# Selective scan: a fourth state of sixteen weighted on GpSimd, and C's rows split as 128x64 tiles

## The reference, cut to what matters

```python
xdbl = jnp.einsum('bld,de->ble', xc, W_xproj)
dt_r, Bm, Cm = xdbl[..., :8], xdbl[..., 8:24], xdbl[..., 24:]
dt = softplus(einsum(dt_r, W_dt) + b_dt)          # 512 steps x 256 channels
def step(h, inp):
    h = h * exp(dt_t[:, :, None] * A) + dt_t[:, :, None] * B_t[:, None, :] * u_t[:, :, None]
    y = jnp.einsum('bdn,bn->bd', h, C_t)          # sum over the 16 states n
    return (h, y)
y = (ys + xc * D_param) * silu(z)
out = x + einsum(y, W_out)
```

## Time and profile before

| | us |
|---|---|
| median of 3 runs (lowest, highest) | 2778.79 (2772.78, 2779.42) |
| the profiled execution's own time | 2771.78 |
| its span | 2770.0 |
| the scan, first recurrence to last weighting (900.4 to about 1330) | some 430 |

### The profile page before, as it was taken

How to read it: one execution, slowest core, us unless ns; L and a number is a source line. 1 busy time by engine, 2 the same in 40 slices (tenths; PEclk the granted TensorE clock), 3 DMA queues, 4 the chain that set the end, 5 groups by cost and what they waited for, 6 DMA issues and landing times. The chain is left out here.

```text
span 2770.0 us, 42642 instructions
## 1 busy us (share of the span) xinstructions
PE 2480.3 (90%) x13253; PEld 1589.3 (57%) x13280; DVE 1740.7 (63%) x4100; ACT 1433.8 (52%) x2908; POOL 1615.9 (58%) x1421
## 2 busy tenths in 40 slices
PE   7977787799578899997579899999999999999999
PEld 4756777687565344433379734444444445777776
DVE  4436444575424999999756599999999992211112
ACT  3431333334246877775334377777777774333333
POOL 4742555442364999999145376777767771997000
PEclk9988999899788999999889999999999999999999
DMA  9011333500012232322520068888888884000001
GB/s 295 25 35 49 109 107 108 165 1 24 26 40 73 93 98 91 96 97 88 175 80 25 14 142 196 192 191 191 191 195 187 194 193 100 9 16 9 8 8 31
DMA packets 148262, 274.82 MB, mean 99 GB/s; under 512 B 29003, under 2 KB 68694, under 8 KB 148038
## 3 DMA queue, kind: packets, MB, share of 16 engines
q1 hardware_dynamic: 135798, 251.75, 35.2%
q0 software_dynamic: 9088, 18.63, 2.4%
q10 hardware_dynamic: 3152, 1.71, 0.3%
HBM read 102.97 MB, written 24.58 MB: 46 GB/s over the span
## 5 line engine op out<-in xcount | busy, mean ns | idle before, releaser
L1784 POOL TENSOR_TENSOR l3a_p_all<-l3a_p_all,l3a_rden 128x1024 f32<-128x1024 f32 x256 | 483.7, 1893 | 202.2 <-DVE l3a_rden L1859 202.1
L1917 ACT ACTIVATE l3a_p_all<-l3a_p_all,l3a_low 128x512 f32<-128x512 f32 x512 | 364.3, 713 | 129.8 <-DVE l3a_low L1854 128.5
L1854 DVE CUSTOM_DVE_ANT_0 l3a_p_all<-bank,relative_bias 128x512 f32<-128x512 f32 x512 | 331.9, 686 | 53.9 <-PE bank L1983 30.5
L1867 DVE STREAM_TRANSPOSE l3a_blocks<-l3a_p_all 128x1024 f32<-128x1024 f32 x256 | 313.9, 1235 | 1.8 <-issue 1.8
L2784 POOL TENSOR_TENSOR l2a_dBu<-l2a_du,l2a_bs 128x1024 f32<-128x1024 f32 x128 | 298.5, 2352 | 17.4 <-DVE l2a_h L3020 16.2
L3020 DVE TENSOR_TENSOR_SCAN l2a_h<-bank,l2a_dBu 128x1024 f32<-128x1024 f32 x128 | 290.9, 2281 | 11.9 <-POOL l2a_dBu L2784 6.5
L1841 DVE SCALAR_TENSOR_TENSOR x<-bank,l3a_blocks,x 128x128 f32<-128x128 f32 x256 | 71.9, 344 | 336.5 <-PE bank L2058 336.3
L1932 ACT ACTIVATE relative_bias<-bank,l3a_b 128x512 f32<-128x512 f32 x224 | 153.3, 687 | 214.1 <-PE bank L2048 210.8
L1983 PE MATMUL bank<-l3a_kT,l3a_qT 64*128 64x512 f32 x1024 | 245.3, 607 | 3.1 <-DVE l3a_low L1854 2.6
L2009 PE MATMUL bank<-l3a_pT,l3a_v 128*64 128x512 f32 x1024 | 233.8, 598 | 0.1
L2048 PE MATMUL bank<-relative_xnT_all,relative_w_qk 128*128 128x512 f32 x512 | 231.0, 595 | 0.0
(11 more groups left out here) (532 smaller groups left out, 4964.3 us busy)
## 6 DMA issues: line engine op xcount, KB each, us to landing
l3a_pT<-l3a_blocks SPq DMA_DIRECT2D x1024, 128.0 KB
l2a_bs<-l2a_b_rows SPq DMA_DIRECT2D x128, 256.0 KB, 3.1
l0fe_wv<-expert_weights SPq DMA_DIRECT2D x71, 256.0 KB
by_place<-by_distance SPq DMA_DIRECT2D x16, 512.0 KB, 12.6
relative_bias<-by_place SPq DMA_DIRECT2D x16, 448.0 KB, 11.3
l2a_c_rows<-l2a_b_rows SPq DMA_DIRECT2D x24, 256.0 KB
expert_weights<-in_L_ffn_in_dram SPq DMA_DIRECT2D x1, 4096.0 KB, 29.1
l0f_answers<-l0f_y_rows SPq DMA_DIRECT2D x16, 256.0 KB, 5.2
```

Source lines behind the costliest of these rows:

```text
L1784: p_ready.by(pool.tensor_tensor(a, a, bcast(rden[g % 2][:, t, :], n_after=S), ALU.mult))
L1854: bk.drain(dve.tensor_tensor_reduce(p_of(g, t)[:, h, :], ps(job)[:], bias[:, u * 2 + h, b0:b0 + S], 1.0, 3.0e38, ALU.add, ALU.min, low[:, ...
L1867: ins = dve.transpose(out, p_of(g, t).rearrange("p h (k b j) -> p (h k) b j", b=Q, j=32))
L1917: ins = act.activation(a, a, ACT.Exp, bias=low[:, t, h:h + 1], scale=-1.0, accum_out=den[:, t, h:h + 1])
```

## The change

- Loads: C's 16 rows are read back from DRAM as one flat 128x64 tile (`c_flat`); SP issues this load for the first block before all, for block q + 1 ahead of the `bs` load of n = 5, and waits there for the store of `b_rows[q + 1]`.
- Splits: the rounding and subtracting run on 128x64, on C alone; three DMAs that ACT issues at n = 12 put the parts into `bc`. Their places in the orders move: ACT n = 1, 6, 11 to 6, 9, 12; POOL n = 5, 10 to 9, 12 (first block 7, 10 to 10, 13). PE's spread waits for these DMAs.
- SHARED becomes (0, 3, 6, 9), added at PE's steps 6, 9, 12, 15.
- POOL's step sizes are done at n = 11 and 12 in place of 12 and 13.

```diff
-        raw, dtr, left, mid = sb("raw", [2 * N, S]), sb("dtr", [R, S]), sb("left", [2 * N, S]), sb("mid", [2 * N, S], BF16)
+        raw, dtr = sb("raw", [2 * N, S]), sb("dtr", [R, S])
+        CUT = N * S // P
+        c_flat, c_left, c_parts = sb("c_flat", [P, CUT]), sb("c_left", [P, CUT]), sb("c_parts", [P, 3, CUT], BF16)
...
-        SHARED, LATER, ADDED_AT = (0, 3, 6), 4, {0: 6, 3: 12, 6: 13}
+        SHARED, LATER, ADDED_AT = (0, 3, 6, 9), 4, {0: 6, 3: 9, 6: 12, 9: 15}
...
+                def load_flat(q):
+                    sp.wait_ge(b_stored, 16 * (q + 1))
+                    if q:
+                        sp.wait_ge(left_ready, q)
+                    sp.dma_start(c_flat[:], b_rows[q, N:2 * N, :].rearrange("n (c s) -> (n c) s", s=CUT)).then_inc(flat_loaded, 16)
+
                 answers.load(sp, (0,))
+                load_flat(0)
                 for m in range(M):
                     q, n = divmod(m, N)
-                    if n == 0:
-                        sp.wait_ge(b_stored, 16 * (q + 1))
+                    if n == 5 and q + 1 < B:
+                        load_flat(q + 1)
...
                 def split_left(q):
+                    pool.wait_ge(flat_loaded, 16 * (q + 1))
                     pool.wait_ge(hi_ready, q + 1)
-                    pool.wait_ge(raw_ready, q + 1)
-                    pool.tensor_tensor(left[:], raw[:], bc[q % 2][0:2 * N, :], ALU.subtract).then_inc(left_ready, 1)
+                    if q:
+                        pool.wait_ge(low_ready, q)
+                    pool.tensor_tensor(c_left[:], c_flat[:], c_parts[:, 0, :], ALU.subtract).then_inc(left_ready, 1)
...
-                        if n == (5 if q else 7):
+                        if n == (9 if q else 10):
                             split_left(q + 1)
-                        if n == 10:
+                        if n == (12 if q else 13):
                             split_last(q + 1)
+                        if n == 11:
+                            add_step(q + 1, slice(0, CH))
                         if n == 12:
-                            add_step(q + 1, slice(0, CH))
-                        if n == 13:
                             weigh_step(q + 1, slice(0, CH))
...
                 def split_done(q):
                     act.wait_ge(left2_ready, q + 1)
-                    act.copy(bc[q % 2][PART:PART + 2 * N, :], mid[:])
-                    act.copy(bc[q % 2][2 * PART:2 * PART + 2 * N, :], left[:]).then_inc(bc_ready, 1)
+                    act.copy(c_parts[:, 2, :], c_left[:]).then_inc(low_ready, 1)
...
+                    for k in range(3):
+                        rows_of_part = bc[q % 2][k * PART + N:k * PART + 2 * N, :]
+                        act.dma_start(rows_of_part.rearrange("n (c s) -> n c s", s=CUT), c_parts[:, k, :]).then_inc(bc_loaded, 16)
...
                 log_dt(0)
-                split_mid(0)
+                split_first(0)
                 deviations(2)
                 turn_to(ACT.Exp)
                 act.wait_ge(held.a_ready, 2)
+                split_mid(0)
...
-                        if n == 1 + late:
-                            split_first(q + 1)
...
-                        if n == 6 + late:
+                        if n == 6 + late // 2:
+                            split_first(q + 1)
+                        if n == 9 + late // 2:
                             split_mid(q + 1)
...
-                        if n == 11 + late:
+                        if n == 12 + late // 2:
                             split_done(q + 1)
...
-                    pe.wait_ge(bc_ready, q + 1)
+                    pe.wait_ge(bc_loaded, 48 * (q + 1))
```

More of the change, by code:

```diff
@@ L2693, in selective_scan @@
         mv_ready, gains_ready, rows_ready, x_normed = sem("mv_ready"), sem("gains_ready"), sem("rows_ready"), sem("x_normed")
-        xc_ready, sz_ready, hi_ready, raw_ready, left_ready, mid_ready, left2_ready, bc_ready = (
-            sem(n) for n in ("xc_ready", "sz_ready", "hi_ready", "raw_ready", "left_ready", "mid_ready", "left2_ready", "bc_ready"))
+        xc_ready, sz_ready, raw_ready, hi_ready, left_ready, mid_ready, left2_ready, low_ready = (
+            sem(n) for n in ("xc_ready", "sz_ready", "raw_ready", "hi_ready", "left_ready", "mid_ready", "left2_ready", "low_ready"))
+        flat_loaded, bc_loaded = sem("flat_loaded"), sem("bc_loaded")
         log_ready, dt_ready, du_ready, exp_order = sem("log_ready"), sem("dt_ready"), sem("du_ready"), sem("exp_order")
@@ L2733, in split_left @@
                 def split_left(q):
+                    pool.wait_ge(flat_loaded, 16 * (q + 1))
                     pool.wait_ge(hi_ready, q + 1)
-                    pool.wait_ge(raw_ready, q + 1)
-                    pool.tensor_tensor(left[:], raw[:], bc[q % 2][0:2 * N, :], ALU.subtract).then_inc(left_ready, 1)
+                    if q:
+                        pool.wait_ge(low_ready, q)
+                    pool.tensor_tensor(c_left[:], c_flat[:], c_parts[:, 0, :], ALU.subtract).then_inc(left_ready, 1)
                 def split_last(q):
                     pool.wait_ge(mid_ready, q + 1)
-                    pool.tensor_tensor(left[:], left[:], mid[:], ALU.subtract).then_inc(left2_ready, 1)
+                    pool.tensor_tensor(c_left[:], c_left[:], c_parts[:, 1, :], ALU.subtract).then_inc(left2_ready, 1)
                 def add_step(q, part):
@@ L2868, in take_bc @@
                     bk.wait_filled(act, job, 0)
-                    if q:
-                        act.wait_ge(left2_ready, q)
                     act.copy(dtr[:], ps(job)[2 * N:2 * N + R, :]).then_inc(dtr_ready, 1)
@@ L2876, in take_bc, with split_mid, split_done @@
                     act.sem_inc(raw_ready, 1)
+                    act.wait_ge(raw_ready, q + 1)
                     act.dma_start(b_rows[q], raw[:]).then_inc(b_stored, 16)
                 def split_first(q):
+                    act.wait_ge(flat_loaded, 16 * (q + 1))
+                    if q:
+                        act.wait_ge(bc_loaded, 48 * q)
+                    act.copy(c_parts[:, 0, :], c_flat[:]).then_inc(hi_ready, 1)
+                def split_mid(q):
+                    act.wait_ge(left_ready, q + 1)
+                    act.copy(c_parts[:, 1, :], c_left[:]).then_inc(mid_ready, 1)
+                def split_done(q):
+                    act.wait_ge(left2_ready, q + 1)
+                    act.copy(c_parts[:, 2, :], c_left[:]).then_inc(low_ready, 1)
+                    act.wait_ge(cleared, 1)
                     if q >= 2:
                         act.wait_ge(C_ready, (q - 1) * len(of_dve) // B)
[L2882 to L2889, removed]
-                    act.copy(bc[q % 2][PART:PART + 2 * N, :], mid[:])
-                    act.copy(bc[q % 2][2 * PART:2 * PART + 2 * N, :], left[:]).then_inc(bc_ready, 1)
+                    act.wait_ge(hi_ready, q + 1)
+                    act.wait_ge(mid_ready, q + 1)
+                    act.wait_ge(low_ready, q + 1)
+                    for k in range(3):
+                        rows_of_part = bc[q % 2][k * PART + N:k * PART + 2 * N, :]
+                        act.dma_start(rows_of_part.rearrange("n (c s) -> n c s", s=CUT), c_parts[:, k, :]).then_inc(bc_loaded, 16)
                 def take_dt(q, j):
@@ L2935, in _ @@
                 take_bc(0)
-                act.wait_ge(cleared, 1)
-                split_first(0)
                 for j in range(CH):
@@ L3140, in add_up @@
                     for j in range(CH):
-                        ins = pe.matmul(y_bank[j][:], chip.ident[:], weighed[:, j, :], start=False, stop=(m % N == N - 1))
+                        ins = pe.matmul(y_bank[j][:], chip.ident[:], weighed[:, j, :], start=False, stop=(m == adds[(m // N + 1) * N - 1]))
                     ins.then_inc(hc_summed, 1)
```

## The result

The changed kernel takes **2792.9 us** (12 runs, 2786.7 to 2799.1) against 2778.1 for the one before (12 runs): +14.8 us, ratio 1.0049, 95% interval 1.0038 to 1.0059. The forecast was slower, 2788.9 in 2772 to 2797; direction and range held, the size was 10 us and came out as 15.

A forecast was written before the change was run, and what follows sets the result against it. It took four about equally busy engines, bound in blocks 2 to 4 by a loop of DVE, PE and ACT. Block 0 with start +5.0, blocks 1 to 5 +4.3, block 6 +1.1, block 7 -0.3: +10.1, giving 2788.9 us (2772 to 2797).

The forecast's parts named there:

- rival C: Block 0: PE idles 6 us behind the missing dBu and turns cold; 2793 to 2797 us, 0.13 of slower cases.
- Rival A: Blocks 2 to 4: PE's clock stays at 1.00, 3.5 us come off; +6.6, 2785 us, chance 0.35.
- What bounds the kernel: Blocks 2 to 4: a loop of DVE, PE's matmuls, ACT; DVE's removed 1.11 us lies beside PE's chain.
- Step 3: Blocks 1 to 5: GpSimd's fourth weighting makes dBu 14 end at 48.2, delaying recurrence 14; +0.85 us each, +4.3 in all.
- step 6: Start: first dBu +0.5 us later; ACT's stores 0.31 each, landing early; finish at n = 1 has 1.8 us of room.
- Step 5: SP's queue: the flat load's wait holds bs loads; nothing in blocks 1 to 6, block 0 with the start +5.0 us.
- Step 4: Block 6: dBu 14 ends at 46.2 where recurrence 14 stood at 45.1, +1.1 us; block 7's finish 0.3 sooner.

The follow-up runs named there:

- run 5: The kernel before with states 0, 3, 6, 9 on GpSimd, added at PE's steps 6, 9, 12, 15, nothing else: 2701.4 us, ratio 1.0029.
- run 7: The changed kernel with three states on GpSimd, flat load at n = 9, step sizes back at n = 12 and 13: 2695.2 us, ratio 1.0008.
- run 4: The changed kernel with 8 matmuls by zeros added on PE at step 3 of block 0: 2793.0 us, ratio 1.0044.
- run 1: The changed kernel with the flat load ahead of the bs load of n = 9 in place of n = 5: 2782.8 us, ratio 1.0012.
- run 3: The kernel before with only SP's wait at n = 5 for the next block's stored rows added: 2783.4 us, ratio 1.0014.

## Why the forecast was right, and where its size was off

In the profile the change cost 15.3 us with the start, where 10.1 were forecast: 3.1 more than forecast in block 0 with the start, 1.7 in blocks 1 to 5, 0.4 in the last two. These didn't cancel; the range held because it reached to rival C (2793 to 2797, 0.13 of the slower cases), whose mechanism did occur in block 0. Rival A's did not: three of blocks 1 to 5 read 0.97 after as before.

**What bounds the kernel.** Held. Taking 1.1 us a block off DVE, its most busy engine, gave nothing, because it lay beside PE's convolution steps (the 0.98 wait at n = 10), and the fourth weighting on GpSimd cost 7.6 us of scan by itself (run 5).

**Step 3 (blocks 1 to 5, +0.85 each).** Right mechanism, too small: 1.2. The waits stand at recurrences 13 and 14, and ACT's at the block's start is gone. In block 3 (0.97) dBu 14 ends at 48.5 where 48.2 was worked out, and 6.63 follow to the next block against 6.7; the term that was mis-sized is the start of the weighting of n = 6, 29.66 in place of 29.37. PE's last add at step 15 holds the spread of n = 1 for 0.27 (step 6 had called this room), and everything behind it in the block is 0.3 to 0.4 later. Run 5 has the same 0.27, and its blocks at 1.00 are the changed kernel's (54.08 to 54.10 against 54.12) without the stores to bc. ACT's stores, priced in step 6 at 0.31 each and hidden, take 0.6 each and do hold z's copy and PE's gate (6.4 us in six waits, in the changed kernel as in run 7). With three states this goes with 0.3 a block; in the changed kernel DVE doesn't wait for ACT at a block's start, and nothing shows that they cost it anything. The forecast that POOL's wait before n = 6 would grow to 2 us in blocks 2 to 4 was wrong in part: it is 1.64 in block 3, at 0.97, and 0.57 and 0.58 in blocks 2 and 4, at 1.00, where PE's add comes earlier.

**Step 5 (SP's queue).** "Nothing" for blocks 1 to 6 was nearly so: POOL waited 0.3 to 2.2 us for bs 5 in each, landing 3.5 in place of 3.1. In blocks 2 to 6 this was won back before dBu 7 or nearly; in block 1 not all (with PE at work, run 4, block 1 is 54.64 against 54.13 in run 1, both at 1.00). For block 0 the stall came as worked out (6.89 of waiting, against 6 to 7), but the block lost 7.6 after its start in place of 4.5. What the sum had left out is the one I made rival C: PE at 0.50 for 11 us, 3.1 us of DVE's time. Runs 1, 3 and 4 show the parts: without the stall block 0 is 8.3 us shorter, with it and PE kept at work 2.9 shorter, which leaves 4.7 over the kernel before, the forecast's 4.5; and the wait alone makes the stall.

**Step 6.** The start cost 0.48, from du to the first recurrence, as said. **Step 4:** block 6 +1.4 against 1.1. The Trainium skill's page DMA: Bandwidth & Descriptors (Anatomy of one DMA) gives a DMA that GpSimd issues about 2.0 us plus bytes / 436e3, an estimated 2.6 us for the 256 KB of a bs load. The page states this fit for GpSimd's path alone, and these loads are issued from SP: they had 3.1 in the median before, 3.5 in the changed kernel and 6.1 at most.

**Left open:** whether ACT's stores cost the changed kernel anything in its blocks at 0.97 (55.14 to 55.27, run 5 54.9 to 55.0; run 5 also has the large splits and the later step sizes); stores from another queue were not tried. In which blocks the clock reads 0.97 and in which 1.00 changes from variant to variant and even between the two profiles of the kernel before; each such block costs some 1.1 us, and I can't say what chooses them.

## What to carry to other kernels

A wait placed in a queue that issues loads in order is a wait of every load behind it: look for the first turn of the loop, where the awaited thing is latest, not for the steady turn. When several engines are about equally busy, ask what the freed engine meets next (here PE's spread, which took 0.98 of the 1.11 back at once) and where the receiver is furthest behind (here dBu 14, for 1.2 us a block). Price a DMA issue on a computing engine by what stands behind it in that engine's order.

## What the hardware showed unexpectedly

An idle PE of 6.9 us was followed by 11 us of work at the 1.2 GHz level (granted 0.50), so a stall upstream was paid again by half: 5.6 us more of waiting for dBu 5 than before (6.89 against 1.26) came with 8.3 us of block 0, 2.9 of which went when PE was kept at work. In the kernel before with only the wait, PE idled 5.6 us and its next add also took 3.62, but the clock was back within 5 us of PE's restart. Three DMA issues in a row on ACT took 1.85 to 2.1 us in the changed kernel, twice what three single ones (0.31) suggest; the first of the three alone took 0.55 and more, and they store other shapes than the single one, so it isn't shown that the row is the reason.
